# A graph layer on one core: in the last block the sums over d move behind the products they add, in three parts

## The reference, cut to what matters

```python
h = relu(layernorm(x))
score = einsum('md,md->m', (h @ W_Q.T)[dst], (h @ W_K.T)[src]) / sqrt(128) * exp(-edge_dt)
# per dst: keep the 16 best scores, alpha = softmax over them
agg[n] = sum over kept edges of alpha * (h[src] @ W_msg.T)
out = x + relu(h @ W_self.T + agg)
```

## Time and profile before

| | us |
|---|---|
| median of 3 runs | 2033.47 |
| lowest and highest | 2032.13 and 2034.27 |
| the profiled execution | 2033.06 |
| its span, first to last instruction | 2031.3 |
| the last block and what follows, from the first product of block 99 | about 38 |

### The profile page before, as it was taken

The page is one execution under the profiler, slowest core; times in us unless marked ns, Lnnn a source line. Parts: engine busy times, 40 slices in busy tenths (PEclk is TensorE's granted clock), DMA queues, the critical chain, the costliest instruction groups (busy, mean ns, idle before and its releaser), DMA issues.

```text
span 2031.3 us, 48459 instructions
## 1 busy us (share of the span) xinstructions
PE 1406.6 (69%) x15213; PEld 1292.2 (64%) x15214; DVE 1488.7 (73%) x5024; ACT 1073.4 (53%) x3376; POOL 1492.5 (73%) x1577
## 2 busy tenths in 40 slices
PE   0047888777677777767777676776776777677776
PEld 0047778667666666666667666665776667566765
DVE  5668999767777677777767767777686777767766
ACT  2667767545454554545555454554554555455553
POOL 6766777777777777777777777777777777777773
PEclk9968999888887888988888888889778887888887
DMA  7933333333333333333333333333333333333321
GB/s 204 278 112 89 105 115 105 99 102 88 100 97 91 101 89 99 92 95 101 86 102 93 95 101 86 101 90 98 101 87 101 86 101 88 97 101 87 99 74 33
DMA packets 120707, 206.67 MB, mean 102 GB/s; under 512 B 32268, under 2 KB 75922, under 8 KB 120252
## 3 DMA queue, kind: packets, MB, share of 16 engines
q0 software_dynamic: 50192, 103.42, 20.0%
q1 hardware_dynamic: 69627, 97.27, 14.9%
q10 hardware_dynamic: 626, 2.84, 0.4%
HBM read 186.96 MB, written 16.44 MB: 100 GB/s over the span
## 4 chain that ended last, share of the span: by engine, by line
DVE 36%; issue 20%; DMA 15%; PE 15%; POOL 6%; ACT 5%; POOLq 2%; SPq 1%; ACTq 0%; DVEq 0%
DVE s L893 10%; DMA X<-H_table,idx 6%; PE pS L1280 5%; DMA Z<-H_table,idx 4%; DVE Dm L917 4%; DVE D L786 4%; DVE X L888 4%; DMA E<-H_table,idx 4%; PE pU L1273 3%; POOL E L608 2%; POOL X L608 2%; ACT X L1146 2%; PE pT L1237 2%; PE pS L1237 2%; POOL Z L608 2%
## 5 line engine op out<-in xcount | busy, mean ns | idle before, releaser
L608 POOL DMA_INDIRECT X<-H_table,idx x662 | 628.3, 949 | 208.2 <-issue 157.2
L1146 ACT ACTIVATE X<-OT,w 128x125 f32<-128x125 bf16 x1792 | 530.1, 386 | 30.2 <-DVE w L967 30.2
L608 POOL DMA_INDIRECT E<-H_table,idx x437 | 414.1, 948 | 141.4 <-issue 112.5
L1118 ACT ACTIVATE OT<-pT 128x512 bf16<-128x512 f32 (+1 forms) x500 | 274.8, 550 | 403.4 <-PE pT L1248 382.7
L608 POOL DMA_INDIRECT Z<-H_table,idx x403 | 382.4, 949 | 125.1 <-issue 93.8
L1248 PE MATMUL pT<-identb,O 125*128 125x128 bf16 x1800 | 212.0, 244 | 309.5 <-DVE X L888 260.4
L1248 PEld LDWEIGHTS pT<-identb,O 125*128 125x128 bf16 x1800 | 134.1, 108 | 361.6 <-issue 279.2
L1237 PE MATMUL pG<-G,O 125*128 125x128 bf16 x3600 | 316.4, 251 | 0.0
L1237 PEld LDWEIGHTS pG<-G,O 125*128 125x128 bf16 x3600 | 278.1, 116 | 0.1
L893 DVE TENSOR_REDUCE s<-X 128x8 f32<-128x1024 f32 x200 | 268.4, 1342 | 0.0
L1273 PE MATMUL pU<-X 128*128 128x125 f32 x1512 | 192.1, 282 | 1.6
(11 more groups left out here) (197 smaller groups left out, 2489.9 us busy)
## 6 DMA issues: line engine op xcount, KB each, us to landing
rawi<-D_table SPq DMA_DIRECT2D x50, 576.0 KB
ewt<-D_table SPq DMA_DIRECT2D x50, 576.0 KB
X<-H_table,idx POOLq DMA_INDIRECT x662
E<-H_table,idx POOLq DMA_INDIRECT x437
Z<-H_table,idx POOLq DMA_INDIRECT x403
hb<-H_table SPq DMA_DIRECT2D x100, 62.5 KB
xb<-in_x SPq DMA_DIRECT2D x100, 62.5 KB
out<-ob SPq DMA_DIRECT2D x100, 62.5 KB
```

Of the source, the lines that this page charges most:

```text
L608: return eng.indirect_dma_start(out=Et[q][:, t * 128:(t + 1) * 128], out_offset=None, in_=x if b < RAW else H, in_offset=bass.IndirectOffs ...
L1118: AT.mark(eng.activation(OT[b % 3][:, q0[g]:q0[g] + GQ[g], :].rearrange("p t n -> p (t n)"), pT[:, 0:GQ[g] * 128], ACT.Copy), b, f"T{g}")
L1146: last = eng.activation(weighted(c)[:, t * 128:t * 128 + NB], OT[c % 3][:, t, 0:NB], ACT.Copy, scale=w[:, t:t + 1])
```

## The change

In blocks 0 to 98 the instructions and their order stay as they are: the two sums are only written in another way. In block 99 there are three sums. The first, r0 over tiles 0 to 7, stands right behind s1; the second, r2 over tiles 8 to 13, behind s3; the third, r1 over tiles 14 to 17, behind s4. Since `islice(now, 3)` takes three instructions whatever they are, the third of them is now r0 and no longer s2.

```diff
+                def sums(name, a, z, behind):
+                    VM.wait(eng, b, behind)
+                    return VM.mark(eng.tensor_reduce(s[:, a:z], junk[:, a * 128:z * 128].rearrange("p (t d) -> p t d", d=128),
+                                                     AX.X, ALU.add), b, name)
...
                     yield VM.mark(eng.tensor_tensor(junk[:, c0:c0 + n], Et[b % NE][:, c0:c0 + n], gx(g)[:, 0:n], ALU.mult), b, f"s{g}")
-                t = 0
-                for k in range(2):
-                    n = RED[k]
-                    VM.wait(eng, b, "s1" if k == 0 else "s4")
-                    yield VM.mark(eng.tensor_reduce(s[:, t:t + n], junk[:, t * 128:(t + n) * 128].rearrange("p (t d) -> p t d", d=128),
-                                                    AX.X, ALU.add), b, f"r{k}")
-                    t += n
+                    if b == B - 1 and g == 1:
+                        yield sums("r0", 0, g0[2], "s1")
+                    elif b == B - 1 and g == 3:
+                        yield sums("r2", g0[2], g0[4], "s3")
+                if b < B - 1:
+                    yield sums("r0", 0, g0[2], "s1")
+                    yield sums("r1", g0[2], T, "s4")
+                else:
+                    yield sums("r1", g0[4], T, "s4")
```

More of the change, by code:

```diff
@@ L7, with __init__ @@
 class Line:
-    def __init__(self, sem, names):
-        self.sem, self.names = sem, names
+    def __init__(self, sem, names, blocks=0, last=None):
+        self.sem, self.names, self.last = sem, names, last or names
+        self.blocks = blocks
         self.done = 0
     def mark(self, ins, b, name):
-        at = b * len(self.names) + self.names.index(name)
+        at = self.at(b, name) - 1
         assert at == self.done, (b, name, self.done)
@@ L20, in at @@
     def at(self, b, name):
-        return b * len(self.names) + self.names.index(name) + 1
+        return b * len(self.names) + (self.last if b == self.blocks - 1 else self.names).index(name) + 1
     def wait(self, eng, b, name):
@@ L49, in gnn_kernel @@
     OC = [0, 6, 12, 18]
-    RED = [8, 10]
     GP = [5, 5, 4, 4]
@@ L249, in gnn_kernel @@
         SEL = ["deg", "pen", "Shm", "Sl", "Sm", "m8a", "top", "mr1", "m8b", "thr", "cnt", "Vh", "Vr", "Vm", "Vl"]
-        VM = Line(sem("VM"), [f"s{g}" for g in range(5)] + ["r0", "r1", "sd", "sh", "sr", "sm", "sl", "sw", "D"])
+        PARTS = ["sd", "sh", "sr", "sm", "sl", "sw", "D"]
+        VM = Line(sem("VM"), [f"s{g}" for g in range(5)] + ["r0", "r1"] + PARTS, B,
+                  ["s0", "s1", "r0", "s2", "s3", "r2", "s4", "r1"] + PARTS)
         VW = Line(sem("VW"), SEL + ["we", "dx", "ge", "w", "rec"])
```

## The result

The changed kernel took 2028.97 us, the median of 22 runs from 2025.68 to 2032.68; the kernel before, in the same comparison, 2032.41 (22 runs, 2027.31 to 2035.80). The ratio is 0.9986 with a 95% interval of 0.9979 to 0.9992, that is 2.8 us or 0.14% faster, between 1.6 and 4.3 us (the two medians alone lie 3.4 us apart). The forecast was 2.41 us and "within 0.2%". The prediction took some 4 us for the least difference that can be told; with 22 runs on each side the interval reaches only about 1.3 us to either side and does not include zero. Single runs of one kernel differ by 7 us and more here, so the place of each microsecond has to be read from the traces. The profiled executions hardly show the gain in their spans, 2031.3 against 2030.9 us: that of the changed kernel is the slowest of its 22 runs (2032.68), and in it output(97) came 1.94 us later.

A forecast was written before the change was run, and what follows sets the result against it. Bound taken: in the last block s2's wait for a gather's landing holds the picks, and TensorE waits behind them. Terms: -2.95 us at Sc plus 0.54 for the last aggregate, -2.41; forecast 2030.9 us, range 2029.4 to 2033.1.

The forecast's parts named there:

- The picks come earlier: VectorE, last block: r0 fills the idle time before s2, so the last pick of block 98 ends 3.37 us earlier.
- TensorE's queue takes part of it back: output(97) stands ahead of the gather of weights, so 1.27 us are lost and w gains 2.1 us.
- D: VectorE behind fin, block 99: with s2 and the cut sums there, D comes 2.33 us earlier, at 2009.16.
- The landing of the last tile: Last gather of block 99: lands 2.52 us after issue, at 2003.70, leaving 0.8 us before s4 asks for it.
- The clock: TensorE in aggregate(98): clock stays full or soon returns, so it takes 4.92 us and D decides when Sc starts; 0.60.
- rival (a): Clock falls as before: aggregate(98) keeps 6.67 us, Sc starts 2.1 us earlier, gain 1.0 to 2.1 us; chance 0.22.
- the -2.95 of the sum: Start of Sc in block 99: at 2009.22, 0.06 us after D, 2.95 us earlier than before.
- The other clock term: Last aggregate, within 3.6 to 7.2 us: takes 6.14 instead of 5.60 after a clock fall, so 0.54 us are lost.
- Rival (b): TensorE stays at 1.2 GHz from 2003 to the end; last aggregate 7.2 us, kernel 1.10 slower, 2034.2; chance 0.06.
- Rival (c): The first sum, r0, holds up POOL's gathers for all its 1.21 us; gain only 2.0 us, 2031.3; chance 0.04.
- Rival (d): Something else holds the picks, or output(97) comes late: no change, 2033.1 to 2033.5 us; chance 0.08.

The follow-up runs named there:

- e2: Kernel before with only the sums cut (8, 6 and 4 tiles, all behind finish(97)), s2 left ahead of the picks: 2033.50 us, ratio 1.0003 to before.
- e3: Kernel before with s2 moved behind finish(97) in the last block and no sum in its place: 2031.48 us, ratio 0.9998 to before.
- e4: Changed kernel with the gather of weights for block 98 ahead of output(97) in TensorE's queue: 2030.65 us, ratio 0.9990 to before.
- e1: Changed kernel with the second sum not cut, its ten tiles added in one sum behind s4: 2030.16 us, ratio 0.9994 to before.
- e8: Changed kernel with the gather of weights for block 98 ahead of output(97) and idle matmuls at three places (4, 11, 11): 2029.24 us, ratio 0.9979.
- second set: Repeat on a chip with usual times; the changed kernel, unedited, took 2032.23 us against 2034.11 before, ratio 0.9989.
- e7b: Changed kernel with idle matmuls: six ahead of aggregate(98), eleven each ahead of gather of weights 99 and aggregate(99), usual chip: 2029.13 us, 0.9978 to before.
- e5: Changed kernel with six idle matmuls between the gather of weights for block 98 and aggregate(98), on the slow chip: ratio 1.0001 to before.
- e6b: Kernel before with seven idle matmuls ahead of the gather of weights for block 98 and six behind it, usual chip: 2034.92 us, ratio 1.0005.
- e7: Changed kernel with idle matmuls at three places (6, 11, 11), on the slow chip: ratio 0.9988 to before.
- e6: Kernel before with seven idle matmuls ahead of the gather of weights for block 98 and six behind it, slow chip: ratio 1.0018.
- e0: Changed kernel run again without edits, on the slow chip: ratio 0.9991 to before.

## Why the prediction was right, and where it was not

**The picks come earlier: right.** Forecast: the sum 0.16 us behind the start of pen, Shm 1.13 behind that, the last pick 3.37 us earlier. Measured: 0.16, 1.13, and 3.33 (from 2.43 after the start of output(97) to 0.90 before it). e2, which keeps s2 in front, has none of it; e3, which only moves s2, has the gather of weights at the same 0.32 (w at 2.13, behind its pause). It is the place of s2 that brings the picks and the gather forward, not the cutting of the sums.

**TensorE's queue takes part of it back: right.** Forecast 2.1 us at w, measured 2.18 (2.17 at the gather). e4 confirmed the reason: with output(97) out of the way w comes 1.02 earlier, where I had expected 0.8.

**D: right.** I expected D 9.28 after the start of output(97) (2009.16 - 1999.88); it was 9.22 in all three profiles of the changed kernel. The sums took 1.21, 0.95 and 0.69 us (forecast 1.21, 0.94 and 0.67). That the cut of the second sum has a small price of its own, e1 shows: 0.19 us.

**The landing of the last tile: mis-sized.** I took 2.52 us from one landing and saw 0.8 us of slack left before s4. But the product that waits starts some time behind the landing: s2 stood 2.74 us behind the start of its gather (1998.93 - 1996.19), so 0.6 us were left by that row. And the landings differ: 2.68 us in e4 and 3.10 in e8, with s4 starting 2.76 and 3.18 us behind the start of the gather. With POOL's last issue at 1.32 s4 can then start at 4.1 to 4.5, and it starts at 4.54 in the changed kernel. It didn't wait in any of the three profiles, but by the latest landing next to nothing is left. Why landings differ, no run shows.

**The clock: this step failed.** "I think the clock stays full or soon comes back. Then aggregate(98) ends at 2003.57 + 4.92 = 2008.49, D at 2009.16 decides" did not happen in any profile of the changed kernel, nor in e1. The clock fell 1.6 to 2.1 us after the start of output(97) each time, aggregate(98) took 6.58 to 6.82, and Sc stood behind it. The argument for a full clock was that the idle 2.01 us before the gather go; with them gone the clock fell sooner, not later. The row that it leaned on was misread, too. I put 0.60 us of work into the 4.5 us ahead of the fall in the kernel before, which leaves the output out; its stretch from the end of aggregate(97) reads

```profile
1999.34:2003.80 4.46, 1.09 (x21) 1.00 0.19 48
```

In the changed kernel it fell after 0.92 us of work in 2.11. The case that came is rival (a), to which I gave 0.22; it gave a gain of 1.0 to 2.1, and 2.3 came: aggregate(98) started 2.19 earlier and took 0.09 less, and the last aggregate lost nothing. So the -2.95 of the sum was -2.27. The other clock term, +0.54 for the last aggregate, was -0.05 (5.55 against 5.60 before). The two errors, 0.68 and 0.59, nearly cancel: -2.41 forecast, -2.31 in the profiles, -2.8 (-4.3 to -1.6) in the runs and -2.2 (-4.3 to -0.4) in the second set. That the total came out so close is luck: one term was too good by what the other was too bad. The bounds of the last aggregate were off as well: at the full clock throughout it took 4.18 us (e7b, e8), not the 3.6 that I had for its least.

**What I tied to the clock was not only a term of size.** I compared a full clock after with a half clock before, and so counted 0.5 us of clock as a gain of the change. e5 and e6b separate the two: the change gives 2.40 at Sc with the full clock on both sides, 2.27 with the half clock on both, and the clock itself gives 0.5 at Sc without the change and 0.65 to 0.9 with it. That the idle matmuls are what keeps the clock is shown as far as 14 profiles can: in the eight without them it fell 1.6 to 4.8 us after the start of output(97), in the six with them not before 14.0 us.

**Rival (b)** did not come true as a whole, but its last part did, in e3 and e4: there the last aggregate took 6.80 and 6.74, and in e4 that ate the 1.1 us that Sc had gained. That a gain at Sc can be lost 10 us later, in a step that no edit touched, is why the last instruction and not Sc has to be read. **Rival (c)**, that the sum holds up POOL, did not come. POOL while the sum ran, from 1996.85 to 1998.06:

```profile
1995.65 0.94 POOL L610 DMA_INDIRECT E<-H_table,idx  x1 [0.30 <-issue]
1996.89 0.95 POOL L610 DMA_INDIRECT E<-H_table,idx  x1 [0.30 <-issue]
1998.14 0.94 POOL L610 DMA_INDIRECT E<-H_table,idx  x1 [0.30 <-issue]
```

Neither the issues nor the steps between them are longer. The prediction holds moving s2 for the more likely disturbance, since it would have two inputs from SBUF; but s2 reads one from SBUF and one from PSUM (`X<-E,pG`). **Rival (d)** was not the case here; on the chip with the early landings its premise held, for a reason I had not thought of: s2 isn't late there.

What stays open is the part of the difference that the runs show beyond the 2.3 us of the last block. It lies within the interval, and in the profiles of the changed kernel and the kernel before on chips with the usual times output(97) started between 1998.67 and 2001.82, behind blocks that no edit touched. What sets the moment at which the clock falls or comes back stays open, too: in three profiles of the same kernel it fell at 1.6, 1.9 and 2.1 us.

## What to carry to other kernels

In an engine that works its queue in order, look for an instruction that waits for a transfer and stands in front of work that needs nothing from it. Moving it is worth at most what the next queue down the path leaves: here the picks won 3.3 us, and TensorE's own order let 2.2 through. Cutting the work behind it into parts gave nothing by itself (e2) and cost 0.19 us at D (e1); whether it pays where the last part waits for a landing, no run shows. In a tail where TensorE idles for some microseconds between short steps, matmuls that nobody needs, placed so that they end before the next real one is ready, can be worth as much as the reordering: e7b, with three groups of them, came 4.5 us under before, the reordering alone 2.2. Where the groups stop at the first step, the last aggregate still runs in part at the lower clock: it took 5.29 us in e5 and 6.33 in e6b, and e6b gained nothing at the end.

## What the runs showed of the hardware

- In the changed kernel the granted clock fell from 2.4 to 1.2 GHz 1.6 to 2.1 us after the start of output(97) in all three profiles; from the end of aggregate(97) to just before the fall TensorE had been busy for 0.92 of 2.11 us in the first of them, with no idle stretch over 0.7 us. With six matmuls more (1.45 us) between the gather of weights and the next step it did not fall before aggregate(98) was done in e5, e7 and e7b, nor in e8 with four (1.03 us), nor in the kernel before with seven and six (e6, e6b).
- An aggregate of 36 passes took 4.18 us at the full clock (the last one in e7b and e8, aggregate(97) in e1 and e3), 4.92 at the full clock where it ran beside ScalarE's scaling of its tiles, and 5.3 to 6.8 where part of it ran at the lower level, the same instructions each time.
- A gather of a tile took 2.48 to 2.52 us from the start of its issue to the landing in the kernel before, e2 and e6b, and 2.68 and 3.10 us for the last tile of the block in e4 and e8.
- On one chip the whole kernel took about 2580 us instead of 2032, yet in the last block w and D stood at the same 1.78 and 9.22 us after the start of output(97) (e0).
